# Cross attention in halves: 32-row and 32-column TensorE tiles, and softmax denominators from matmuls with ones

## The reference, cut to what matters

```
xn = layernorm(x)                                  # over the 128 features
q, k, v = xn @ Wq + bq, ctx @ Wk + bk, ctx @ Wv + bv
s = (q_h . k_h) / sqrt(8)                          # 16 heads, 128 x 77 each
s = where(mask == 0, -big, s)                      # layer 2: one mask row per sequence
p = softmax(s)                                     # layer 5: a 128 x 77 mask per sequence
x = x + concat_h(p @ v_h) @ Wo + bo
```

## Time and profile before

| | us |
|---|---|
| median of 2 runs | 3027.53 (3022.42 to 3032.64) |
| the profiled execution | 3026.77 |
| its span, first to last instruction | 3025.0 |
| layer 2 (cross attention, one mask row) | about 1137 to 1500 |
| layer 5 (cross attention, full mask) | about 2401 to 2719 |

### The profile page before, as it was taken

One profiled execution on the slowest core, in us unless ns is written; L12 is line 12 of the kernel. 1 busy time (PEld: TensorE's weight loads), 2 busy tenths in 40 slices (PEclk: granted clock), 3 DMA queues, 4 the chain that ended last, 5 costly groups with the idle time before them and its releaser, 6 DMA issues. The chain is left out here.

```text
span 3025.0 us, 44993 instructions
## 1 busy us (share of the span) xinstructions
PE 2610.4 (86%) x12704; PEld 1694.9 (56%) x12704; DVE 2333.7 (77%) x3947; ACT 1473.6 (49%) x2681; POOL 1452.5 (48%) x1216
## 2 busy tenths in 40 slices
PE   2888787788778767999879998799999899997997
PEld 0333333333333335666568887466666577775776
DVE  3999999999999986777545555588888699984555
ACT  3666676666667633444332222466666445442000
POOL 4666666666666766555510000455555566652000
PEclk8999999999999998999969999899999999997999
DMA  2000000000000001000000000000000100000000
GB/s 62 1 1 1 0 1 0 1 0 0 0 0 0 1 0 69 4 4 4 20 1 1 1 0 5 1 0 0 0 0 0 39 9 8 8 5 1 7 10 11
DMA packets 30806, 20.88 MB, mean 7 GB/s; under 512 B 18102, under 2 KB 29408, under 8 KB 30192
## 3 DMA queue, kind: packets, MB, share of 16 engines
q1 hardware_dynamic: 30704, 19.71, 2.3%
HBM read 17.60 MB, written 2.10 MB: 7 GB/s over the span
## 5 line engine op out<-in xcount | busy, mean ns | idle before, releaser
L783 POOL TENSOR_TENSOR m_hc<-m_h,m_cs 128x1024 f32<-128x1024 f32 x256 | 603.1, 2358 | 351.3 <-DVE m_h L705 346.7
L705 DVE TENSOR_TENSOR_SCAN m_h<-m_da,m_pdb 128x1024 f32<-128x1024 f32 x256 | 585.0, 2285 | 25.0 <-DVE m_pdb L660 6.8
L456 PE MATMUL m_py<-m_hc,ident 128*128 128x512 f32 x1024 | 513.7, 626 | 4.2 <-DVE m_y L669 2.1
L579 ACT ACTIVATE m_da<-m_dt,m_aneg 128x508 f32<-128x508 f32 x512 | 337.9, 709 | 46.1 <-POOL m_dt L752 44.4
L660 DVE TENSOR_TENSOR m_pdb<-m_du,m_pdb 128x1024 f32<-128x1024 f32 x256 | 314.7, 1229 | 39.6 <-POOL m_du L759 11.4
L456 PEld LDWEIGHTS m_py<-m_hc,ident 128*128 128x128 f32 x1024 | 201.6, 199 | 212.5 <-issue 174.0
L978 ACT ACTIVATE x_prT<-x_pt 77x512 f32<-77x512 f32 x256 | 151.8, 593 | 316.5 <-PE x_pt L894 316.5
L1121 POOL TENSOR_TENSOR x_pr<-x_pr,x_rden 128x308 f32<-128x308 f32 x256 | 179.4, 701 | 196.1 <-DVE x_rden L1043 195.4
L920 PE MATMUL x_py<-x_prT,x_va 77*32 77x128 f32 x2048 | 271.0, 276 | 0.0
L594 ACT ACTIVATE m_cs<-m_pc 128x512 f32<-128x512 f32 x256 | 150.5, 588 | 220.1 <-PE m_pc L446 220.1
L442 PE MATMUL m_pdb<-m_bcrow,m_sel 96*128 96x512 bf16 x256 | 102.5, 400 | 175.4 <-DVE m_h L705 174.4
(11 more groups left out here) (250 smaller groups left out, 5784.2 us busy)
## 6 DMA issues: line engine op xcount, KB each, us to landing
cw_gu<-in_C_gu SPq DMA_DIRECT2D x1, 2304.0 KB
x<-in_x SPq DMA_DIRECT2D x8, 256.0 KB, 5.5
fw_w<-in_F_w SPq DMA_DIRECT2D x1, 2048.0 KB
out_x<-x SPq DMA_DIRECT2D x8, 256.0 KB, 2.3
x_mrow<-in_B_mrow SPq DMA_DIRECT2D x1, 1232.0 KB, 6.0
x_ctxT<-in_B_ctxT SPq DMA_DIRECT2D x32, 38.5 KB, 1.8
x_ctxT<-in_E_ctxT SPq DMA_DIRECT2D x32, 38.5 KB, 1.8
x_mask<-in_E_mask SPq DMA_DIRECT2D x32, 38.5 KB, 1.8
```

Of the source, the lines that this page charges most:

```text
L456: ins = mm(py[:, c, :], S.ident[:, :], hc[n % BUF][:, place(n, c), :], start=n == 0, stop=n == NS - 1)
L579: A_(dst, src, ACT.Exp, scale=aneg[:, d, c, n:n + 1]).then_inc(s["da_ready"], 1)
L705: V.tensor_tensor_scan(h[n % BUF][:, way], da[n % BUF][:, d:d + CH * GT][:, way], pdb[:, b:b + 2, :].rearrange("p c t -> p (c t)")[:, way] ...
L783: P.tensor_tensor(hc[n % BUF][:, :, :], h[n % BUF][:, :].rearrange("p (c t) -> p c t", c=CH), bc(cs[n % BUF][:, :], 1, CH), ALU.mult).then ...
```

## The change

The layer is rewritten for halves of a sequence (`Half`, `walk_halves`: two slots per sequence, `h` = 0 and 1, eight heads each).

- **Scores.** `kd` holds four heads' worth of keys, not sixteen: `hm4` keeps of each 32-feature block one head. The scores of a quad are a matmul over the 32 features of its own block (`rows`), two quads of a half into two banks of `ps`. Masks of both layers are now an added bf16 matmul behind them: layer 2 with ones over the same 32 rows, layer 5 with the bf16 identity over 128 rows. `madd` is made by VectorE once per sequence.
- **Softmax.** One maximum, one subtraction, one exponential per half (616 elements). The sum (L1030), the inversion (L1043) and GpSimd's multiplication (L1121) go. The transposed exponentials are multiplied with `va` and, in 16 more float32 matmuls, with `unit`, a matrix of ones in `va`'s layout, which puts each head's denominator beside its context. VectorE inverts a 128 x 128 tile once per sequence and multiplies.
- **Order of values.** All 32 matmuls of a sequence stand together, and the four quads alternate in the inner loop, so that neighbours go to different 32-column tiles.
- **Beside that.** The bias of v moves to GpSimd, the copy of v to ScalarE; `bn_aggr` on VectorE and one GpSimd power per sequence replace `ln_scalars`; zeroing of `va` moves to GpSimd; layer 2's mask rows (L863) are loaded with the layer's weights, in the first layer; `py` has one buffer, not two.

```diff
@@ tensor engine
+                def turn(u):
+                    pe.wait_ge(s["exp_ready"], u.k + 1)
+                    for e in range(Q2):
+                        if due(Q2 * (u.k - 1) + e + 1):
+                            pe.wait_ge(s["prT_ready"], Q2 * (u.k - 1) + e + 1)
+                        for i in range(QH):
+                            ins = tr(pt[e][0:TC, i * T:(i + 1) * T], pr[u.p][u.h][:, QH * e + i, :], S.ident[:, :])
+                        ins.then_inc(s["pt_mm"], 1)
+                def scores(u):
...
+                    for e in range(Q2):
+                        rows = slice(32 * (Q2 * u.h + e), 32 * (Q2 * u.h + e) + 32)
+                        mm(ps[u.h][:, e, 0:QK], qT[u.p][rows, :], kd[u.p][rows, :, :], start=True, stop=False)
+                    for e in range(Q2):
+                        rows = slice(32 * (Q2 * u.h + e), 32 * (Q2 * u.h + e) + 32)
+                        if full_mask:
+                            ins = mm(ps[u.h][:, e, 0:QK], S.ident_bf[:, :], bc(madd[u.p][:, :], 1, QH),
+                                     start=False, stop=True)
+                        else:
+                            ins = mm(ps[u.h][:, e, 0:QK], ones[rows, :], bc(madd[u.p][rows, :], 1, QH),
+                                     start=False, stop=True)
+                    ins.then_inc(s["s_mm"], 1)
+                def values(b):
+                    pe.wait_ge(s["prT_ready"], NQ * (b.n + 1))
...
                     for i in range(QH):
+                        for q in range(NQ):
+                            mm(pyo[W4 * q:W4 * q + W4, 0:T], va[b.p][:, q, W4 * i:W4 * i + W4],
+                               prT[b.p][q][:, i * T:(i + 1) * T], start=i == 0, stop=i == QH - 1)
                     for i in range(QH):
+                        for q in range(NQ):
+                            ins = mm(pyo[W4 * q:W4 * q + W4, 2 * T:3 * T], unit[:, W4 * i:W4 * i + W4],
+                                     prT[b.p][q][:, i * T:(i + 1) * T], start=i == 0, stop=i == QH - 1)
                     ins.then_inc(s["y_mm"], 1)
+                def project_out(b):
+                    pe.wait_ge(s["cT_ready"], b.n + 1)
+                    mm(pyo[:, T:2 * T], cT[:, :], W.wo[:, :], start=True, stop=True).then_inc(s["o_mm"], 1)
+                def slot(u):
+                    last = u.seq.plus(-1)
+                    if u.real():
+                        turn(u)
+                    if u.plus(2).real():
+                        scores(u.plus(2))
+                    if u.h == 0:
+                        if u.seq.plus(2).real():
+                            project_in(u.seq.plus(2))
+                        if last.real():
+                            values(last)
+                    else:
+                        if last.real():
+                            project_out(last)
+                        if u.seq.plus(3).real():
+                            turn_x(u.seq.plus(3))
@@ vector engine
+                def slot(u):
+                    a = u.plus(2)
+                    m, n, o = u.seq.plus(2), u.seq.plus(3), u.seq.plus(-1)
                     if a.real():
+                        sc = ps[a.h][:, :, 0:QK].rearrange("p e (i k) -> p e i k", k=TC)
+                        dve.wait_ge(s["s_mm"], a.k + 1)
...
+                        V.tensor_reduce(top[a.p][a.h][:, :].rearrange("p (e i) -> p e i", i=QH), sc, AX.X, ALU.max
+                                        ).then_inc(s["top_ready"], 1)
+                    if u.h == 1 and o.real():
+                        dve.wait_ge(s["y_mm"], o.n + 1)
...
+                        V.reciprocal(rden[:, :], pyo[:, 2 * T:3 * T]).then_inc(s["rden_ready"], 1)
+                        dve.wait_ge(s["rden_ready"], o.n + 1)
...
+                        if full_mask:
+                            V.tensor_tensor(cT[:, :], rden[:, :], pyo[:, 0:T], ALU.mult).then_inc(s["cT_ready"], 1)
+                        else:
+                            V.scalar_tensor_tensor(cT[:, :], rden[:, :], some[:, bass.ds(o.n, 1)], pyo[:, 0:T],
+                                                   ALU.mult, ALU.mult).then_inc(s["cT_ready"], 1)
                     if a.real():
+                        dve.wait_ge(s["top_ready"], a.k + 1)
...
+                        V.tensor_tensor(pr[a.p][a.h][:, :, :].rearrange("p (e i) k -> p e i k", i=QH), sc,
+                                        bc(top[a.p][a.h][:, :].rearrange("p (e i) -> p e i", i=QH), 3, TC),
+                                        ALU.subtract).then_inc(s["sub_ready"], 1)
```

More of the change, by code:

```diff
@@ L790, in _, with __init__, plus, real @@
                 drive(pool, front, scan, par)
+class Half:
+    def __init__(self, j, p, h):
+        self.seq = Seq(j, p)
+        self.n, self.p, self.h = self.seq.n, p, h
+        self.k = 2 * self.n + h
+    def plus(self, k):
+        b = self.seq.plus((self.h + k) // 2)
+        return Half(b.j, b.p, (self.h + k) % 2)
+    def real(self):
+        return self.seq.real()
+def walk_halves(eng, slot, ahead):
+    turns = (ahead + 1) // 2
+    def both(j):
+        for p in range(2):
+            for h in range(2):
+                slot(Half(j, p, h))
+    for j in range(-turns, 1):
+        both(j)
+    with eng.Fori(1, NB // 2 - turns) as j:
+        both(j)
+    for j in range(NB // 2 - turns, NB // 2 + 1):
+        both(j)
 def cross_weights(nc, ctx, w, full_mask):
@@ L799, in cross_weights @@
     W.hmask = W.tile("hmask", [128, HX], w["hmask"])
+    if not full_mask:
+        W.mrow = W.tile("mrow", [128, NB * TC], w["mrow"].partition_broadcast(128), I32)
     return W
@@ L961, in _ @@
+                walk_halves(pe, slot, 3)
             @block.scalar
@@ L997, in _ @@
+                walk_halves(act, slot, 3)
             @block.vector
@@ new lines, in moments @@
+                def moments(lo, hi):
+                    for b in range(lo, hi):
+                        ins = V.bn_aggr(mv[:, b, :], S.bn[:, b, :])
+                    ins.then_inc(s["aggr"], 1)
+                    dve.wait_ge(s["aggr"], 1 if lo == 0 else 2)
+                    V.tensor_scalar(ve[:, lo:hi], mv[:, lo:hi, 1], LN_EPS, None, ALU.add).then_inc(s["ve_ready"], 1)
+                moments(0, EARLY)
+                dve.wait_ge(W.loaded, W.all())
+                V.tensor_scalar(bqs[:, :], W.bq[:, :], SCALE, None, ALU.mult).then_inc(s["bqs_ready"], 1)
@@ L1090, in slot @@
-                    if q == 3 and o.real():
+                            dve.wait_ge(mask_in[m.p], 16 * (m.j + 1))
+                            ints = mask[m.p][:, :]
+                        else:
+                            ints = W.mrow[:, bass.ds(m.n * TC, TC)]
+                        if due(Q2 * (m.n - 1)):
+                            dve.wait_ge(s["s_mm"], Q2 * (m.n - 1))
+                        V.tensor_scalar(madd[m.p][:, :], ints, 0.0, MASKED, ALU.is_equal, ALU.mult
+                                        ).then_inc(s["madd_ready"], 1)
@@ L1126, in slot @@
+                P.memset(unit[:, :].rearrange("p (i x) -> p i x", x=VSTEP)[:, :, 0:DKX], 1.0
+                         ).then_inc(s["unit_ready"], 1)
+                def slot(u):
+                    c, m, r = (u.seq.plus(k) for k in (1, 2, 4))
+                    if u.h == 1 and m.real():
+                        if isinstance(m.n, int) and m.n == 0:
+                            pool.wait_ge(s["hm4_ready"], 1)
                         pool.wait_ge(s["q_ready"], m.n + 1)
-                        if due(NQ * (m.n - 2) + q + 1):
-                            pool.wait_ge(s["s_mm"], NQ * (m.n - 2) + q + 1)
@@ L1136, in slot @@
                                         ).then_inc(s["xb_ready"], 1)
-                walk_sequences(pool, slot, 3)
+                walk_halves(pool, slot, 3)
 def moe_top2_weights(nc, ctx, w):
```

349 lines of the change are left out of this document (129 added, 220 removed).

## The result

| | before | after |
|---|---|---|
| median of 2 runs, us | 3027.53 | 3292.04 (3289.69 to 3294.39) |
| the profiled execution, us | 3026.77 | 3289.69 |
| its span, us | 3025.0 | 3287.9 |
| mean granted TensorE clock | 0.950 | 0.831 |
| distance of two contexts, layer 2 / 5, us | 10.66 / 9.37 | 14.61 / 14.54 |

The changed kernel is slower: 1.0878 of the time before, interval [1.0842, 1.0915]. The forecast was 2970 us.

A forecast was written before the change was run, and what follows sets the result against it. TensorE was taken to set the pace: 9.15 us per sequence in layer 2, 9.54 in layer 5; 42 - 5 + 12 + 6 = 55 us off 3026.8 gave 2972, rounded to 2970. The 8-in-10 range was 2918 to 3078.

The forecast's parts named there:

- The bound before: Both layers of the kernel before: TensorE sets the pace, at 10.66 and 9.37 us per sequence and clock 1.00.
- Values and denominators: TensorE, once per sequence: 64 narrow records, four column tiles running together, 1.91 us with shape change and first load.
- Scores and masks of a half: TensorE, each half: two overlapping quads plus masks, 1.18 us in layer 5, including 0.15 for uncovered weight loads.
- Transposes: TensorE, sixteen per sequence: 0.88 us per eight, 0.15 more for the half after narrow values, 1.91 in all.
- Projections with what follows them: TensorE, the three projections of each sequence: 0.62 us, as before the change.
- The inversion: VectorE, 128 x 128 tile once per sequence, inside TensorE's wait: 0.95 us, picked between 0.30 and 1.29.
- cheap: Rival: VectorE's inversion takes only 0.30 us, 38 us less in total, 2932 us; chance 0.22.
- The wait: TensorE idle once per sequence at h = 1, from its scores to VectorE's `cT`: 1.41 us plus 0.95 inversion.
- The clock: Rival: TensorE's new wait lowers its clock, adding about 5% to 7.2 us of own work, 2993 us; chance 0.10.
- The Mamba row: Profile row of the Mamba layer: PE busy 426 of 540 us at granted clock 0.96, used to price a lowered clock.
- the block of values over 2.8 us: Sign of being wrong, on TensorE's values per sequence; from 2.8 us on the 55 us gain is used up.
- `madd` is just in time: VectorE's mask tile ends 1.1 us after `cT`; TensorE needs it 1.26 us after, so no second wait.

The follow-up runs named there:

- before_wait: Kernel before, with one unneeded TensorE wait per sequence, after the scores at q = 1 for VectorE's subtraction: 3389.73 us.
- filled_wait: Changed kernel plus twenty useless identity transposes in TensorE's gap, ahead of the output projection: 2996.07 us.
- ctx_first: Changed kernel with VectorE's inversion and context multiplication moved ahead of its wait for the scores: 2881.14 us.
- ctx_mask_first: ctx_first with VectorE's mask tile `madd` also made ahead of the wait for the scores: 2840.46 us, 0.9379 of the kernel before.
- inv_first: Changed kernel with only VectorE's inversion moved ahead of its wait for the scores; the multiplication stays behind the maximum: 2963.63 us.
- filled_elsewhere: Changed kernel plus twenty useless identity transposes ahead of the input projections, where TensorE doesn't wait: 3236.51 us.
- serial_tiles: Changed kernel with the loops of values swapped, so eight matmuls in a row go to the same 32-column tile: 3509.1 us.
- no_wait_serial: ctx_mask_first with the loops of values swapped, so eight matmuls in a row go to the same 32-column tile: 2980.82 us.

## Why the prediction was wrong

**The bound before** was read rightly: TensorE, with nothing to wait for. `before_wait` shows it from the other side, since one added wait goes to the end in full and more.

**TensorE's own work** came out by its terms, where the clock is 1.00. Values and denominators: forecast 1.91, measured 1.88 and 1.89; four column tiles do run at once. Scores and masks of a half: 1.18 forecast in layer 5, 0.99 measured, or 1.08 with the 0.09 for the change of shape that stands in the transposes' row; of the 0.15 for uncovered weight loads about 0.10 shows. Transposes: 1.91 forecast, 1.03 + 0.97 = 2.00 measured, which holds twice these 0.09. Projections with what follows them: 0.62 forecast, 0.72 measured (2427.40 to 2428.12). The inversion: 0.95 forecast and 0.949 measured, so "cheap" falls. That hit is partly luck: 0.95 was a point picked between 0.30 and 1.29, and the 6.3 ns per element of the last section is neither of the two paces considered. The wait: by its pieces 1.41 + 0.95 = 2.36; in the timeline from the end of the mask's columns, about 1291.74 + 0.13, to 1294.38, 2.51; DVE starts 0.30 after them and not 0.20. `filled_wait`, where the gap is full and the clock stays up, has 9.47 and 9.55 against 9.15 and 9.54. The hit in layer 5 is partly luck too: without a wait the own work is 6.92, not 9.54 - 2.36 = 7.18, and the wait adds 2.63, not 2.36. The 2996 us of that run against 2970 is what the forecast was off by in all but the clock.

**The step that failed is the clock.** The sum took it at full speed, so at nothing, and the rival "The clock" priced it at 23 us with a chance of 0.10. The prediction saw the idle stretch and named the mechanism, then took its price from the Mamba layer's 0.96: "about 5% to 7.2 us of own work", 2993 us. The runs show a clock of 0.53 and 0.56. The contexts lie 14.61 and 14.54 us apart where the filled gap has 9.47 and 9.55: about 5.1 us per sequence, over 28 + 28 intervals 283 us, and 12 more over the last three of both layers; the two spans, 3287.9 and 2994.3, lie 294 apart. That the wait takes the clock down, and not the narrow matmuls alone, is shown from four sides: taken away (`ctx_first`, `ctx_mask_first`), shortened (`inv_first`), filled against moved filling (`filled_wait`, `filled_elsewhere`), and put into the old kernel (`before_wait`). Whether the narrow matmuls keep a fallen clock down for longer is not shown; see below.

One of the prediction's own signs of being wrong came up as well, the block of values over 2.8 us: 3.57 at half clock. It was meant for tiles that don't run at once, and it tells of the clock.

The Mamba row was a poor witness, for it is a mean over another pattern of work and waits: in its 540 us of the trace before, the clock stands at 0.50 for 3.4 or 6.8 us at a time, behind waits of up to 3.5 us, and is soon back. The rows near at hand, both layers at 1.00, said nothing about a layer with a gap. The same trace also had a long fall, 34.1 us at 0.50 at the start of layer 2 (1129.2 to 1163.3), where TensorE was busy for 16.0 of them; the rows of the prediction begin behind it. A cost that no row bounds from above should have widened the range to half speed, which costs a doubling of the own work: 7.2 us more per sequence and 64 sequences would have been 460 us above the forecast.

**The wait was also taken as a part of the change.** The prediction counted 2.36 us of it in every sequence, but it is a matter of DVE's order alone. Without it the same matmuls give 6.95 and 6.92, and the version is 187 us faster than the kernel before, where the change as made is 265 slower.

**Other claims.** "`madd` is just in time" was too kind by some: with the context moved, it is what TensorE waits for, 0.8 and 1.1 us. "Work taken from DVE and ACT is worth nothing" holds as long as TensorE has work.

**What stays open** is how long the clock stays down, and so how much a wait costs. The measured waits and clocks, from the first context to the 29th, with the stretches at 0.50 that begin there:

| kernel, layer | longest wait, us | clock | stretches at 0.50, us |
|---|---|---|---|
| `ctx_mask_first`, 2 and 5 | none | 0.955, 1.000 | none, none |
| `ctx_first`, 2 and 5 | 0.8, 1.1 | 1.000, 1.000 | none, none |
| `inv_first`, 2 and 5 | 1.2, 1.2 | 0.912, 0.896 | 37.5, 3.4, 3.4; 10.2, 44.4 |
| `filled_elsewhere`, 2 and 5 | 2.3, 2.2 | 0.834, 0.852 | 3.4 to 6.8, both |
| `before_wait`, 2 and 5 | 2.2, 2.9 | 0.700, 0.862 | 6.8 to 30.7; 3.4 to 6.8 |
| `serial_tiles`, 2 and 5 | 2.3, 2.2 | 0.582, 0.549 | 3.4 to 112.6; 81.9 to 102.4 |
| changed kernel, 2 and 5 | 2.3, 2.2 | 0.533, 0.562 | 95.6 to 109.2; 3.4 to 112.6 |

(0.955 comes from the fall that began ahead of the layer's first context and lasted to 1190.6.) The three upper rows go with the length of the wait; the four lower ones don't. In them the clock falls again and again, and they differ in how soon it is back. One pair varies that with the wait as it is: in layer 2 twenty transposes more per sequence (`filled_elsewhere`) bring 95.6 us down to 6.8. The long stretches of the table, over 31 us, are all in kernels with this change's matmuls and without those transposes. That hints that such matmuls bring a fallen clock back late, as the 18.2 busy us at 0.50 in `ctx_mask_first` do, but no run puts the wait into a kernel with this change's order and wide matmuls, so it is not shown.

## What to carry to other kernels

Read the granted clock beside PE's busy share, for every stage, before and after: an engine that is 84% busy at 0.53 has lost nearly half its speed, here to a repeated wait of 2.3 us. Look also at how long the clock stands at 0.50 each time, not only at its mean. Where an edit puts one repeated wait into the order of a TensorE that had none, price it from the wait up to a doubling of TensorE's own work in that stage, and look first whether the instruction waited for can be issued ahead of the other engine's own wait. Filling such a gap with useless transposes told within one run that the clock was the loss (3292 to 2996 us).

## What the runs showed of the hardware

- One gap of about 2.3 us in each 15 us went with 1.2 GHz for 95.6 us on end, though PE was busy 85% of them; TensorE got 6.8 us of 2.4 GHz, and the clock fell again in the next wait. In another kernel it stood at 1.2 GHz for 18.2 us in which TensorE was never idle (`ctx_mask_first`, start of layer 2). The Trainium skill (TensorE: Matmul & The Clock Gate, A second HAM failure mode: psum-queue depth-cycling) says that small idle times between groups of matmuls can make the clock go back and forth between its two levels. The trace agrees, with 0.50 and 1.00 and nothing else in the stretches of layer 2 above.
- Four 32-column float32 tiles run at once: 64 records of 128 columns in 1.88 us, 29 ns a record, where records of one tile in a row start 0.11 us apart. The 62 ns per matmul that the prediction cited from the Trainium skill (TensorE: Matmul & The Clock Gate, Wait — 56ns, not 53.3ns?) doesn't bound such a row if each record is counted, as the prediction did; counted as 32 float32 matmuls it is 59 ns each, just under the page's figure, so these runs can't exclude such a limit for whole matmuls.
- Records of different column tiles overlap without being interleaved in the program: 4.25 us for 64, with starts out of the program's order. The Trainium skill (TensorE: Matmul & The Clock Gate, The mechanism) says that matmuls start and end strictly in program order. The starts in the rows of `no_wait_serial` differ from that, and so does the block's length (4.25, where starts in order would need over 6), which doesn't hang on single records.
- An inversion of 128 elements per partition takes 949 ns and one of four took 171: 778 / 124 = 6.3 ns for each further element, against 1.1 for the maximum (800 ns for 616 elements, 463 for 308). The long one reads a PSUM tile and the short one an SBUF tile, so a part of the 778 may be due to that.
